# A batched transformer kernel: M's rotation by two half operations, and softmax sums inverted by way of three transfers

## The reference

```python
xn = layernorm(x)
x  = x + gqa_attention(xn) + ffn_block(xn)      # layer 0
#   gqa_attention: 16 query heads, 4 key/value heads            ("A" in the kernel)
#   ffn_block: t = xn + mla(rmsnorm(xn)); t + moe(rmsnorm(t))   (mla is "M": q and k rotated, causal;
#              k, v from a latent of 64 channels; moe: 4 experts of 512 hidden, the best one per token)
xn = layernorm(x)
x  = x + mqa_attention(xn) + swiglu(xn)         # layer 1
#   mqa_attention: 16 query heads, one key/value head            ("B"); swiglu: 384 hidden
# rotation of a head: concat([x1*cos - x2*sin, x1*sin + x2*cos]), x1 and x2 the two halves of 8 channels
# attention: softmax(q k^T / sqrt(8)) v, then the output projection
```

## Time and profile before

| | |
|---|---|
| median of 3 runs | 2979.12 us (2971.29 to 2981.47) |
| the profiled execution: its own time | 2984.29 us |
| its span, first to last instruction | 2982.5 us |
| TensorE busy | 2787.7 us (93%) |
| VectorE busy | 2351.8 us (79%) |
| ScalarE busy | 1748.6 us (59%) |
| GpSimd busy | 1038.6 us (35%) |
| DMA queue of SyncE | 95.83 MB, 10.5% of 16 engines' time |
| granted clock of TensorE | 0.98 over the span, 1.00 from 1201 to 1379 us |

### The profile page before, as it was taken

One profiled execution on the slowest core, in us unless ns is written; L12 is line 12 of the kernel. 1 busy time (PEld: TensorE's weight loads), 2 busy tenths in 40 slices (PEclk: granted clock), 3 DMA queues, 4 the chain that ended last, 5 costly groups with the idle time before them and its releaser, 6 DMA issues.

```text
span 2982.5 us, 116966 instructions
## 1 busy us (share of the span) xinstructions
PE 2787.7 (93%) x49280; PEld 1459.4 (49%) x49280; DVE 2351.8 (79%) x5811; ACT 1748.6 (59%) x3425; POOL 1038.6 (35%) x2006
## 2 busy tenths in 40 slices
PE   4979999999999999999999999999999999999978
PEld 1345454645545455454645545454454545545442
DVE  4768788797887978889797887979788797887835
ACT  1725656566565665656566565666656566565734
POOL 4243432334343333432334342233433333343110
PEclk7999999999999999999999999999999999999987
DMA  3010101101010010101101010110101001010000
GB/s 115 6 54 23 54 23 31 34 24 54 24 46 19 23 58 24 55 23 32 34 23 54 27 50 12 38 44 23 54 24 39 26 23 57 25 54 19 8 23 5
DMA packets 117452, 103.30 MB, mean 35 GB/s; under 512 B 19990, under 2 KB 116160, under 8 KB 116672
## 3 DMA queue, kind: packets, MB, share of 16 engines
q1 hardware_dynamic: 116928, 95.83, 10.5%
HBM read 8.56 MB, written 4.19 MB: 4 GB/s over the span
## 4 chain that ended last, share of the span: by engine, by line
PE 73%; DVE 19%; issue 4%; ACT 3%; POOL 1%; SPq 0%; DMA 0%; ACTq 0%; DVEq 0%; POOLq 0%
PE bank L526 52%; PE pv L644 17%; DVE mx L844 9%; PE bank L532 2%; PE bank L654 1%; DVE hid L949 1%; DVE hid L955 1%; DVE xn L741 1%; ACT hid L1078 1%; DVE bn L726 1%; DVE bank L849 1%; DVE latn L741 1%; ACT probs L1045 1%; DVE factored L741 1%; DVE l1bn L726 0%
## 5 line engine op out<-in xcount | busy, mean ns | idle before, releaser
L1045 ACT ACTIVATE probs<-bank 128x512 f32<-128x512 f32 x2688 | 1479.3, 597 | 855.6 <-PE bank L526 849.3
L844 DVE TENSOR_REDUCE mx<-bank 128x1 f32<-128x512 f32 x2048 | 1282.2, 682 | 81.4 <-PE bank L526 71.4
L849 DVE CUSTOM_DVE_ANT_0 bank<-bank,mask 128x128 f32<-128x128 f32 (+3 forms) x1024 | 480.4, 515 | 97.8 <-PE bank L526 97.6
L1192 POOL TENSOR_SCALAR_AFFINE_SELECT probs<-probs 128x256 f32<-128x256 f32 (+1 forms) x640 | 230.1, 362 | 765.8 <-ACT probs L1045 759.1
L526 PE MATMUL bank<-kp_B,qp_B 72*32 72x512 bf16 x4096 | 440.0, 394 | 28.7 <-DVE mx L844 24.5
L526 PE MATMUL bank<-kp_A,qp_A 72*32 72x512 bf16 x4096 | 403.7, 382 | 40.9 <-DVE mx L844 31.7
L526 PE MATMUL bank<-qp_B,kp_B 74*32 74x512 bf16 x4096 | 430.2, 384 | 1.4 <-ACT probs L1045 1.0
L526 PE MATMUL bank<-qp_A,kp_A 74*32 74x512 bf16 x4096 | 408.1, 382 | 0.5 <-ACT probs L1045 0.5
L526 PE MATMUL bank<-kp_M,qp_M 72*32 72x128 bf16 (+3 forms) x4096 | 332.7, 307 | 21.2 <-issue 16.0
L644 PE MATMUL pv<-probs,vv_B 128*32 128x512 f32 x2048 | 281.8, 601 | 9.3 <-ACT probs L1045 9.0
L526 PE MATMUL bank<-r2T,w1s 128*32 128x512 f32 x2048 | 281.1, 597 | 4.0 <-DVE hid L922 2.0
(11 more groups left out here) (144 smaller groups left out, 3276.8 us busy)
## 6 DMA issues: line engine op xcount, KB each, us to landing
qp_M<-parts_q SPq DMA_DIRECT2D x144, 128.0 KB
kp_M<-parts_k SPq DMA_DIRECT2D x144, 128.0 KB
qp_A<-parts_q SPq DMA_DIRECT2D x144, 128.0 KB
qp_B<-parts_q SPq DMA_DIRECT2D x144, 128.0 KB
kp_A<-parts_k SPq DMA_DIRECT2D x144, 32.0 KB
xs<-x SPq DMA_DIRECT2D x16, 256.0 KB, 3.1
out<-res SPq DMA_DIRECT2D x16, 256.0 KB, 2.2
kp_B<-parts_k SPq DMA_DIRECT2D x144, 8.0 KB
```

The source lines that it names most:

```text
L844: v.tensor_reduce(mx[:, g % 2, at:at + 1], s1[BANK[a, g, u]][:], AX.X, ALU.max) \
L849: v.tensor_tensor_reduce(bank[:, 0:keys], bank[:, 0:keys], mask[:, SEQ - keys:SEQ], 1.0, LOWEST, ALU.add, ALU.max, mx[:, g % 2, at:at + 1] ...
L1045: act.activation(probs[:, slot, :], s2[BANK2[a, g, u]][:], ACT.Exp).then_inc(sig[f"{a}_exp"], 1)
L1192: pool.affine_select(out=v, in_=v, compare_op=ALU.is_ge, fill=0.0, base=0, pattern=pattern, channel_multiplier=-1).then_inc(sig["M_masked" ...
```

## The change

It has two parts and new times for the table.

**Rotation.** The second projections of `m_q` and `m_k` go, with their weights. VectorE reads the one bank three times: once with the cosines over 128 partitions, and twice over 64 partitions with the sines, each half written to the other half's partitions of `rope_s`.

**Inverses.** `out_turn` and `o_turn` go, with `otok` and `oT`. The attention's result stays in `osb` with channels on partitions, and the output projection reads both halves of `osb` by weights spread over the 128 rows (zeros where `osb` has sums or zeros). In their place, for each pair: `sums_out` transfers the 8 rows of sums to 128 x 32 elements, VectorE inverts these (`sums_inverted`), `inverses_out` transfers them to DRAM, `inverses_in` transfers them back, each row repeated for the 16 rows of its head, to `rcb`, and GpSimd multiplies `osb` by `rcb` in place (`out_scaled`). The three transfers are SyncE's.

```diff
+nms=1.15, nmT=1.5, lag=1.986, pv_M=3.37, pv=3.444, out_copy=1.188, sums=0.15, inverted=0.41, inverses=0.56, spread=0.8, scaled=1.142, o_proj=1.3,
-nms=1.15, nmT=1.5, lag=1.986, pv_M=3.37, pv=2.826, out_copy=1.188, out_turn=0.183, o_turn=0.145, o_proj=0.382,
...
-                put(e + T["out_turn"], "out_turn", a, g // 2)
-        e += T["out_turn"] + T["o_turn"]
-        put(e, "o_turn", a)
+                put(e + T["sums"], "sums_out", a, g // 2)
+                put(e + T["inverted"], "sums_inverted", a, g // 2)
+                put(e + T["inverses"], "inverses_out", a, g // 2)
+                put(e + T["spread"], "inverses_in", a, g // 2)
+                put(e + T["scaled"], "out_scaled", a, g // 2)
         put(e + T["o_proj"], "o_proj", a)
...
+            def sums_out(b, a, g):
+                sp.wait_ge(sig[f"{a}_osb"], total(b, f"{a}_osb", g + 1))
+                sp.dma_start(sums[:, g, :], osb[HD:P:VHALF, g, :]).then_inc(sig[f"{a}_sums"], 16)
+
+            def inverses_out(b, a, g):
+                sp.wait_ge(sig[f"{a}_rc"], total(b, f"{a}_rc", g + 1))
+                sp.dma_start(inverses[g].rearrange("h (c n) -> (h c) n", n=32), rc[:, g, :]) \
+                    .then_inc(sig[f"{a}_rc_out"], 16)
+
+            def inverses_in(b, a, g):
+                sp.wait_ge(sig[f"{a}_rc_out"], total(b, f"{a}_rc_out", 16 * (g + 1)))
+                for s_last, value in last_user(b, turn_rcb, 0, f"{a}_scaled", g + 1):
+                    sp.wait_ge(s_last, value)
+                sp.dma_start(rcb[:], inverses[g].unsqueeze(1).broadcast_to([2 * GROUP, VHALF, SEQ])) \
+                    .then_inc(sig[f"{a}_rcb"], 16)
...
             def m_q(b):
-                for j, wn in enumerate(("m_wq", "m_wqs")):
-                    dense(misc_bank(b, "rope_dve", 1 + j), P, wc(wn), xrT[:], "mq_ps")
+                dense(misc_bank(b, "rope_dve", 3), P, wc("m_wq"), xrT[:], "mq_ps")
...
             def o_proj(b, a):
-                pe.wait_ge(sig[f"{a}_oT"], total(b, f"{a}_oT"))
+                pe.wait_ge(sig[f"{a}_scaled"], total(b, f"{a}_scaled"))
                 for t in range(TILES):
-                    ins = in_columns(m[:, P * t:P * t + P], oT[:, P * t:P * t + P], wc(f"{a.lower()}_wo"))
+                    for g in range(TWOS):
+                        ins = in_columns(m[:, P * t:P * t + P], osb[:, g, P * t:P * t + P],
+                                         wc(f"{a.lower()}_wo")[:, P * g:P * g + P], g == 0, g == TWOS - 1)
...
+                for to in range(0, P, P // 2):
+                    at = P // 2 - to
+                    v.scalar_tensor_tensor(out=rope_s[to:to + P // 2, :], in0=m[at:at + P // 2, :], scalar=factor,
+                                           in1=rot[at:at + P // 2, 1, :], op0=ALU.mult, op1=ALU.mult) \
+                                               .then_inc(sig["rope_dve"], 1)
...
+            def sums_inverted(b, a, g):
+                v.wait_ge(sig[f"{a}_sums"], total(b, f"{a}_sums", 16 * (g + 1)))
+                v.reciprocal(rc[:, g, :], sums[:, g, :]).then_inc(sig[f"{a}_rc"], 1)
...
             def out_copy(b, a, g):
-                for s_last, value in last_user(b, turn_osb, g % 2, f"{a}_ot_ps", g + 1):
+                for s_last, value in last_user(b, turn_osb, g % 2, f"{a}_o_ps", 1):
...
+            def out_scaled(b, a, g):
+                pool.wait_ge(sig[f"{a}_rcb"], total(b, f"{a}_rcb", 16 * (g + 1)))
+                pool.tensor_tensor(osb[:, g, :], osb[:, g, :], rcb[:], ALU.mult).then_inc(sig[f"{a}_scaled"], 1)
```

More of the change, by code:

```diff
@@ L68 @@
 _at = 0
-for _n, _w in (("a_wq", 128), ("a_wk", KCH["A"]), ("a_wv", 32), ("a_wo", 128),
-               ("m_wq", 128), ("m_wqs", 128), ("m_wdkv", LATENT), ("m_wo", 128), ("gate", EXPERTS),
-               ("b_wq", 128), ("b_wk", KCH["B"]), ("b_wv", HD), ("b_wo", 128)):
+for _n, _w in (("a_wq", 128), ("a_wk", KCH["A"]), ("a_wv", 32), ("a_wo", TWOS * 128),
+               ("m_wq", 128), ("m_wdkv", LATENT), ("m_wo", TWOS * 128), ("gate", EXPERTS),
+               ("b_wq", 128), ("b_wk", KCH["B"]), ("b_wv", HD), ("b_wo", TWOS * 128)):
     WCOLS[_n] = (_at, _at + _w)
@@ L218, with kernel_program @@
 LAST = 2
-def kernel_program(nc, x, w_all, w_lat, v_all, r_all, w1, w2, wi_up, wi_down, rope, out):
+def kernel_program(nc, x, w_all, w_lat, v_all, r_all, w1, w2, wi_up, wi_down, rope, inverses, out):
     table = ordered()
@@ L289, in kernel_program @@
         osb = sb("osb", [P, 2, SEQ])
+        sums = sb("sums", [P, 2, 32])
         rc = sb("rc", [P, 2, 32])
-        otok = sb("otok", [P, TILES, D])
-        oT = sb("oT", [P, SEQ])
+        rcb = sb("rcb", [P, SEQ])
         lg = sb("lg", [P, TILES, EXPERTS])
@@ L348, in kernel_program @@
             declare(f"{a}_osb", TWOS)
[L349 removed]
+            declare(f"{a}_sums", 16 * TWOS)
             declare(f"{a}_rc", TWOS)
[L351 to L353 removed]
+            declare(f"{a}_rc_out", 16 * TWOS)
+            declare(f"{a}_rcb", 16 * TWOS)
+            declare(f"{a}_scaled", TWOS)
             declare(f"{a}_o_ps", 1)
@@ L565, in m_k @@
                 pe.wait_ge(sig["latT_ready"], total(b, "latT_ready"))
-                for j in range(2):
-                    dense(misc_bank(b, "rope_dve", 3 + j), P, wl[:, P * j:P * j + P], latT[:], "mk_ps")
+                dense(misc_bank(b, "rope_dve", 6), P, wl[:, 0:P], latT[:], "mk_ps")
             def values(b, src, weight, width, done, name):
@@ L768, in rope_mul @@
                     v.wait_ge(s_last, value)
-                for j, dst in enumerate((full[s[1]], rope_s)):
-                    v.wait_ge(sig[f"{s}_ps"], total(b, f"{s}_ps", j + 1))
-                    if j:
-                        for s_last, value in last_user(b, turn_full, "rope_s", f"{s}_full", 1):
-                            v.wait_ge(s_last, value)
-                    v.scalar_tensor_tensor(out=dst[:], in0=misc[SPARE["rope_dve", first + j]][:],
-                                                  scalar=factor, in1=rot[:, j, :], op0=ALU.mult, op1=ALU.mult) \
-                                                      .then_inc(sig["rope_dve"], 1)
+                v.wait_ge(sig[f"{s}_ps"], total(b, f"{s}_ps"))
+                m = misc[SPARE["rope_dve", first + 2]]
+                v.scalar_tensor_tensor(out=full[s[1]][:], in0=m[:], scalar=factor, in1=rot[:, 0, :],
+                                       op0=ALU.mult, op1=ALU.mult).then_inc(sig["rope_dve"], 1)
+                for s_last, value in last_user(b, turn_full, "rope_s", f"{s}_full", 1):
+                    v.wait_ge(s_last, value)
+                for to in range(0, P, P // 2):
[3 more added lines that the diff above has]
+                                               .then_inc(sig["rope_dve"], 1)
             def m_q(b):
@@ L1258, with by_banks @@
     a = {n: np.asarray(v) for n, v in inputs.items()}
-    swap = np.arange(D) ^ (HD // 2)
     q_at = HD * (np.arange(P) % HEADS) + np.arange(P) // HEADS
     k_at = {"A": HD * (np.arange(KCH["A"]) % KV0) + np.arange(KCH["A"]) // KV0, "B": np.arange(KCH["B"])}
-    pair, head, odd, ch_of = np.unravel_index(np.arange(D), (TWOS, GROUP, 2, HD))
-    o_at = HD * (GROUP * (2 * pair + odd) + head) + ch_of
+    def by_banks(wo):
+        heads = wo.reshape(TWOS, 2, GROUP, HD, D).transpose(2, 1, 3, 0, 4)
+        rows = np.zeros((GROUP, 2, VHALF, TWOS, D), np.float32)
+        rows[:, :, :HD] = heads
+        return rows.reshape(P, TWOS * D)
     def attn(n):
@@ L1301 @@
     sin = sin * np.where(ch < half, -1.0, 1.0)[:, None]
-    rope = np.stack([cos[q_at], sin[q_at]], axis=1).astype(np.float32)
+    rope = np.stack([cos[q_at], sin[q_at ^ half]], axis=1).astype(np.float32)
     nc = bacc.Bacc("TRN2", target_bir_lowering=False, num_devices=1)
```

103 lines of the change are left out of this document (36 added, 67 removed).

## The result

| | before | after |
|---|---|---|
| median of 4 runs | 2979.3 us (2971.3 to 2981.5) | 3139.1 us (3115.1 to 3154.1) |
| profiled execution: span | 2982.5 us | 3125.1 us |
| mean granted clock of TensorE | 0.980 | 0.933 |
| at half clock, over the span | 117.4 us, 12 stretches | 421.2 us, 53 stretches |

The ratio is 1.0534, with a 95% interval of 1.0453 to 1.0615: the change makes the kernel 5.3% slower. I had forecast 1.1% faster.

The account below looks back on a forecast made before the run. TensorE was taken to set the time, with stretches where VectorE does. Terms -38.3 - 16.6 - 8 + 7.7 + 11.2 + 5 + 6.6 = -32.4 us gave 2947 us, 1.1% less, range 2908 to 2990.

Parts of the forecast that it names:

- The cuts on TensorE: Transposes of osb and otok removed, projections doubled, less what VectorE's full stretch hides: -38.3 us.
- Idle time ahead of the transposes: TensorE's 9.7 + 2.0 us of waiting before the removed transposes; as projections now wait for GpSimd, -8 us taken.
- The second projections, -16.6 us, and VectorE's halves at nothing: First stretch of a batch: dropping q's and k's second projections gives 0 to -33.2, middle taken; VectorE's added half operations free.
- the cover: From q's rotation to latn: one half operation (0.60) more, 0.28 + 0.42 us of inversion and product less.
- The port: GpSimd's product beside xn stops a second VectorE operation: 0 or 15.4 us, half taken, +7.7; the skill's rule says +15.4.
- B's projection: GpSimd's product stands behind a mask, so TensorE waits 0.7 us per batch: +11.2 us, bounds 0 and 20.
- The waits that the projection moves: VectorE waits longer for the projection before adding the residual: +5 us for M, at most 17; nothing for B.
- Steps of one place I cost at nothing: Shifts of steps by one place in the table were taken to cost 0.
- The three transfers, hidden: Sums out, inverses out and in: tightest at M's second pair, 10.75 us against 11.1, hidden, barely.
- The third rival: Transfers come late: store and load take half as long again, GpSimd and TensorE wait, sum +38, 3017 us; chance 0.10.
- The end of the last batch: Nothing hides the transfers there: projection starts 8.7 us after the copy's end, not 3.2, and takes 1.07 more: +6.6, once.
- What would show it: Signs: TensorE busy 2713 us, rcb waits near zero, idle before projections near 11 us; wrong if idle falls or grows over 50.

Follow-up runs that it names:

- old_rotation_latn_early: Changed kernel with the rotation from before, residual's start and A's first product moved, 427 bank numbers, latn four maxima earlier, B's projection 0.12 units later: 2921.2 us, ratio 0.9801.
- before_latn_early: Kernel before with two places moved: residual's start away from xn, and latn four maxima earlier as its own step; 2961.8 us, ratio 0.9952.
- three_fixed: Changed kernel with residual's start and the product of A's first pair moved away from xn, and 427 bank numbers per iteration: 3008.6 us, ratio 1.0096.
- the last two kernels: Changed kernel with products moved, 427 bank numbers, latn earlier, B's projection 0.12 units later: 2942.0 us with its new rotation, 2921.2 with the old (few other places differ).

## Why the prediction was wrong

**The step that failed is the sum itself: it has no term for TensorE's clock.** The granted clock was 1.00 in all stretches of the earlier trace rows, and I took every duration of TensorE as given. The profiled execution was to take 2951.9 us and took 3126.8, 175 more. The clock takes 133 of them. The other failed part is idle time: with 75.0 us of cuts, a sum of -32.4 allows it to rise by 43, and it rose by 90. The cuts themselves were right, 80 us at full speed.

Point by point:

- *The cuts on TensorE, -38.3 us.* Right in size. The doubled projection costs 98.5 - 51.2 = 47.3 us against 51.2. With the same two corrections of places, the old rotation and the new inverses (`old_rotation_latn_early`) are 41 us under the old inverses (`before_latn_early`). That this is so near 38.3 is partly luck: it is 55 us of work and 9 of idle time less, and 23 more lost to the clock, and a few smaller places differ too.
- *Idle time ahead of the transposes, -8.* The 11.7 us are gone, but ahead of the projections stand 36.3 us, where I named about 11.
- *The second projections, -16.6 us, and VectorE's halves at nothing.* This step has the wrong sign. The rotation alone costs +47 us in the kernel before, +16 in `three_fixed`, and +21 between the last two kernels, where a few places differ as well. In the kernel before it is the clock that costs (+50 us lost), in the other two pairs TensorE's idle time (+31 and +39). I said that the cover is gone if the halves cost more than 0.7 us each. They last 0.688, but I looked at the duration and not at the distance between starts: 0.96 us for the third operation where 0.60 was in the sum. And the cover that I named, on the way to `latn`, was not where it is paid: TensorE stands for the bank that the rotation reads, then for that of the next maximum, both ahead of `latn`.
- *The port, +7.7 us.* The mechanism was right: the four `xn` take 3.04 us in the batch shown, as foreseen for two that stand, and the rule of the Trainium skill that I held against the row was the better guide, since `xn` takes 45.4 us where it took 33.0: 12.4 in all. The price was not. The same stand alone costs 49 us (36 to 79) in the kernel before, so the upper bound of 15.4 was no bound.
- *B's projection, +11.2 us.* Right: 0.83 to 0.84 us in fourteen batches against 0.7.
- *The waits that the projection moves, +5.* VectorE's wait before it adds M's output rises from 9.3 to 30.0 us, 21 where I took 5 and bounded at 17; for A it rises from 6.5 to 26.5 and for B, where I took nothing, from 2.7 to 38.8. (The 9.3 and 6.5 are in the trace of the kernel before, not in the earlier trace rows.) Most of this waiting costs nothing: `old_rotation_latn_early` has 29.4, 25.9 and 28.2 us of it and is faster than the kernel before.
- *"Steps of one place I cost at nothing."* No run tests them apart. What a run does price is a thing that I had not read: the count of users of the banks, 422 for 433, which falls out of the removed steps. 49 us in the changed kernel, where the stand is 1.63 us, and 19 alone, where it is 0.67.
- *The three transfers, hidden.* Mostly right. GpSimd's 126.7 us of waits for `rcb` are not the near zero that I named as the sign, but little of it reaches TensorE: 30.6 us, of which the very end holds 9.5 and ten of B's places 0.83 each. At four more of B's places TensorE stands as long, and the profile puts it down to a maximum. The third rival gave 3017 us by a mechanism that is not the one at work.
- *The end of the last batch, +6.6 us.* The projection starts 8.8 us after the copy's end (3118.09 - 3109.28), against 8.7 in the sum; it then takes 3.64 us instead of the 2.2 of the sum, at the lower clock:

```profile
3108.68 0.60 ACT L1050 ACTIVATE osb<-pv 128x512 f32<-128x512 f32 x1 [1.19 <-PE pv L662]
...
3118.09 3.64 PE L546 MATMUL bank<-w,osb 128*32 128x128 f32 x64 [9.48 <-POOL osb L1190]
```

- *What would show it.* I named a busy time of 2713 us, 75 less, and a rise of idle time by over 50 us as the sign of error. That sign came: idle time rose by 90. But the busy time rose too, to 2840, and for that I had no sign.
